# Mixer: the norms' sums of squares of two projection pieces taken by four TensorE column groups at once, from a square tile of twice the size

## The chip, the cores and the metric

The kernel runs on one core of a Trainium2 chip. The core has TensorE (matmuls, from SBUF into PSUM), VectorE, ScalarE, GpSimd and SyncE, which here only starts DMAs. Each engine works through its own list of instructions in order, and the engines meet at semaphores. The metric is the device time of one execution in microseconds, the median of the runs shown. Everything is 32-bit float; in the trace each matmul of this type leaves two weight loads and two MATMUL records.

## The reference, cut to what matters

A decoder layer: x + mixer(norm(x)), then cross attention, then a mixture-of-experts feed-forward. Only the mixer is touched. It is a state recurrence over time, of 4 batches of 1024 tokens:

```python
bc = jnp.einsum('bti,oi->bto', value, W_bc).reshape(Bsz, Tlen, H, 4, N)
bc = bc / (jnp.sqrt(jnp.sum(bc * bc, axis=-1, keepdims=True)) + EPS)
Bz, Bx, Cz, Cx = (bc[..., 0, :], bc[..., 1, :], bc[..., 2, :], bc[..., 3, :])
...
z = S[..., None] * (z - dtE * A[None, :, :, None] * s + dtE * (Bz_t[..., None] * u_t[:, :, None, :]))
s = s + dtE * z + dtE * (Bx_t[..., None] * u_t[:, :, None, :])
y = jnp.einsum('bhn,bhnd->bhd', Cz_t, z) + jnp.einsum('bhn,bhnd->bhd', Cx_t, s)
```

H = 32 heads, N = 32 states, 16 value elements a head. The second line is what the change is about: for every token and head the four vectors Bz, Bx, Cz, Cx are divided by their lengths, for which the sum of squares over the 32 states is needed.

## The kernel before, in words

`attention` first projects the inputs (to about 290 us), then runs `mixer` (to about 2090 us); cross attention and the feed-forward follow. The mixer cuts the 1024 tokens of each batch into 16 time chunks of 64 (u = 0 to 15; 4 batches x 64 tokens = 256 columns, UT) and the heads into 4 groups (gp = 0 to 3). A group of a chunk has the running number n = 4u + gp, 0 to 63.

**Projection in pieces.** The vectors of a group come from `value` in four pieces (i = 0 to 3), running number p = 4n + i. Pieces 0 and 1 are the one half of the group's heads (Bz with Bx, then Cz with Cx), pieces 2 and 3 the other half. `projected` on TensorE writes a piece, 2 x 256 columns, into one of two PSUM slots of `ring` (L603, 8 matmuls). `projected` on ScalarE copies the slot into `bc` (L756) and squares it into `sq` (L759), one tile for all pieces. `summed` on TensorE (L617) multiplies the squares with a selection matrix `sel` that adds up 32 states per head: two matmuls of 256 columns, one for each of the piece's two vectors. Each writes a strip of 32 rows of `ssp`, c = 2(i % 2) + v, so pieces 0 and 2 go to strips 0 and 1, pieces 1 and 3 to strips 2 and 3; the first half of the heads starts the accumulation, the second ends it. A strip of 32 rows is a column group of the array: 128 rows by 32 columns of weights. After piece 3 ScalarE takes root, logarithm and exponential (`norms`, L766 to L770), VectorE multiplies (`factors`, L942), and SyncE sends the factors to DRAM and, spread over the partitions, back into `fb` and `fc`.

**Semaphores of this part.** `ring_full` (a piece is in PSUM), `sq_ready` (it is squared, and the slot is free for piece p + 2), `sums_done` (`sq` may be written again, and the norms may be taken), `nr_root` (the root has read `ssp`, so the next group may start its sums).

**The order of the work.** Each engine's order is written out by hand. On TensorE a group of the loop does: `inputs_turned` (L628, transposes, waits for `in_ready` of VectorE's L969), pieces 0 and 1 of the group three further on, the sum of piece 0, at a chunk's start `outputs` of the chunk before (L690), `causal_products` (L641), piece 2, sum 1, piece 3, sum 2, the first quarter of `mixed_states` (L661), sum 3, the rest of `mixed_states` (L661, L671), `mixed_values` (L681). The sums thus trail the pieces by one, with other work between a projection and its sum. Before the loop the pieces of groups 0 to 2 are projected alone. VectorE works through `evolve` (L916, L922: 64 dependent steps a chunk for the next chunk), `inputs` (L955 to L969), `read_out` (L977 to L994), `mask` (L1002, waits for `causal_products`), `post` (L1014 to L1024, waits for `mixed_values`), in an order of its own, up to two groups ahead of TensorE. SyncE's list of loads follows VectorE's and TensorE's signals (L462 to L507).

Of the kernel before, what the change touches and what calls it, by code (L numbers as in the profile page):

```python
# [10 lines left out]
ACT = mybir.ActivationFunctionType  # L11
AX = mybir.AxisListType

P = 128
B, T, DM = 4, 1024, 256
NTOK = B * T
DI, H, N, DH = 512, 32, 32, 16
# [3 lines left out]
UT = CH * L  # L21
# [310 lines left out]
GP = G // 2  # L332
# [3 lines left out]
def mixer(nc, d, st, wbc, x, x1):  # L336

    with ExitStack() as ctx:
        def sb(name, shape, dt=F32):
            return ctx.enter_context(nc.sbuf_tensor(name, shape, dt))  # L340

        def ps(name, shape):
            return ctx.enter_context(nc.psum_tensor(name, shape, F32))

        def sem(name):
            return ctx.enter_context(nc.semaphore(name))

        ident = sb("ident", [P, P])
        sel = sb("sel", [P, G, H])
# [19 lines left out]
        sg = sb("sg", [P, 4, UT])  # L369
        xs = sb("xs", [P, 2, DM])  # L370
        bc = sb("bc", [P, GP, 4, 2, UT])
        sq = sb("sq", [P, 2, UT])
        nr = sb("nr", [P, UT])
        pq = sb("pq", [P, 2, UT])
        fb = sb("fb", [P, 2, 2, UT])
# [9 lines left out]
        ssp = ps("ssp", [P, 512])  # L385
# [26 lines left out]
        sq_ready = sem("sq_ready")  # L412
        sums_done = sem("sums_done")
# [22 lines left out]
        def turns(v):  # L436

            return v.rearrange("p (t b) -> p t b", b=B)
# [149 lines left out]
        def _(pe):  # L588
# [15 lines left out]
                                       start=(k == 0), stop=(k == 3))  # L604
                mm.then_inc(ring_full, 1)

            def summed(u, gp, i):

                n = GP * u + gp
                p = 4 * n + i  # L610
                g, first = 2 * gp + i // 2, 2 * (i % 2)
                pe.wait_ge(sq_ready, p + 1)
                if i == 0 and n > 0:
                    pe.wait_ge(nr_root, n)
                for v in range(2):
                    c = first + v
                    mm = pe.matmul(ssp[H * c:H * c + H, 0:UT], sel[:, g, :], sq[:, v, :],  # L617
                                   start=(i < 2), stop=(i >= 2))
                mm.then_inc(sums_done, 1)

            def inputs_turned(u, gp):
                n = GP * u + gp
                pe.wait_ge(in_ready, n + 1)
                if n > 0:
                    pe.wait_ge(km_ready, n)
                for v in range(2):
                    for b in range(B):
                        mm = pe.transpose(kp[:, v, b * P:(b + 1) * P],  # L628
                                          turns(bc[:, gp, v].rearrange("p i t -> p (i t)"))[:, :, b], ident[:])
                    mm.then_inc(bt_full, 1)  # L630
# [16 lines left out]
            def mixed_states(u, gp, more, un, gn):  # L647
                n = GP * u + gp
                pe.wait_ge(hpad_ready, 2 * n + 2)
                if gp == 0:  # L650
                    pe.wait_ge(dub_in, 16 * (u + 1))
                    if u > 0:
                        pe.wait_ge(x1_ready, u)
                else:
                    pe.wait_ge(post_ready, n)
                for b in range(B):
                    for i in range(2):
                        for v in range(2):
                            for j in range(J):
                                r = slice(N * j, N * j + N)  # L660
                                pe.matmul(yp[r, b * L:(b + 1) * L], hpad[r, v, i, b, :],  # L661
                                          turns(bc[r, gp, 2 + v, i, :])[:, :, b],
                                          start=(b == 0 and i == 0 and v == 0), stop=False, skip_group_check=True)
                    if b == 0 and more:
                        summed(un, gn, 3)
                for v in range(2):
                    for b in range(B):
                        for j in range(J):
                            q0 = (gp * J + j) * 2 * DH
                            o = yp[N * j:N * j + N, UT + v * P:UT + (v + 1) * P]  # L670
                            pe.matmul(o.rearrange("p (i b e) -> p b i e", i=2, b=B)[:, b],  # L671
                                      btt[:, v, b, N * j:N * j + N], dub[:, b, q0:q0 + 2 * DH],
                                      start=False, stop=True, skip_group_check=True)
# [21 lines left out]
            for gp in range(GP - 1):  # L695
                for i in range(4):
                    projected(0, gp, i)
                    if gp > 0 or i > 0:
                        summed(0, gp - (i == 0), (i - 1) % 4)
            summed(0, GP - 2, 3)  # L700
            for u in range(NU):
                for gp in range(GP):
                    un, gn = (u, GP - 1) if gp == 0 else (u + 1, gp - 1)
                    more = un < NU
                    inputs_turned(u, gp)
                    if more:
                        projected(un, gn, 0)
                        projected(un, gn, 1)
                        summed(un, gn, 0)
                    if gp == 0 and u > 0:  # L710
                        outputs(u - 1)
                    causal_products(u, gp)
                    if more:
                        projected(un, gn, 2)
                        summed(un, gn, 1)
                        projected(un, gn, 3)
                        summed(un, gn, 2)
                    mixed_states(u, gp, more, un, gn)
                    mixed_values(u, gp)
            outputs(NU - 1)  # L720
# [2 lines left out]
        def _(act):  # L723
# [26 lines left out]
            def projected(u, gp, i):  # L750
                n = GP * u + gp
                p = 4 * n + i
                g, first = 2 * gp + i // 2, 2 * (i % 2)
                act.wait_ge(ring_full, p + 1)
                o = ring[:, p % 2, :].rearrange("p (v t) -> p v t", v=2)
                nc.scalar.copy(bc[:, gp, first:first + 2, i // 2, :], o).then_inc(bc_ready, 1)  # L756
                if p > 0:
                    act.wait_ge(sums_done, p)
                nc.scalar.activation(sq[:], o, ACT.Square).then_inc(sq_ready, 1)  # L759

            def norms(u, gp):
                n = GP * u + gp
                act.wait_ge(sums_done, 4 * n + 4)
                if n > 0:
                    act.wait_ge(fac_out, 16 * n)
                nc.scalar.activation(nr[:], ssp[:, 0:UT], ACT.Sqrt).then_inc(nr_root, 1)  # L766
                act.wait_ge(nr_root, n + 1)
                nc.scalar.activation(nr[:], nr[:], ACT.Ln, bias=epsb[:, 0:1]).then_inc(nr_log, 1)
                act.wait_ge(nr_log, n + 1)
                nc.scalar.activation(nr[:], nr[:], ACT.Exp, scale=-1.0).then_inc(nr_ready, 1)  # L770
# [28 lines left out]
            for u in range(NU):  # L799
                for gp in range(GP):  # L800
                    un, gn = (u, GP - 1) if gp == 0 else (u + 1, gp - 1)
# [1310 lines left out]
```

## Time and profile before

| | us |
|---|---|
| median of 3 runs | 3287.18 |
| the runs | 3287.13, 3287.18, 3292.7 |
| the profiled execution | 3292.7 |
| its span, first to last instruction | 3290.8 |
| TensorE busy in the span | 2934.3 (89%) |
| VectorE busy | 2066.6 (63%) |
| ScalarE busy | 1308.5 (40%) |
| mean granted TensorE clock | 0.936 |

The profile is of one execution, and it is the longest of the three shown. Busy times are averages over stages with different limits: the mixer is some 1800 us of the span. TensorE's records overlap, so the time of a block of matmuls is read from its first weight load to the next line's first weight load, not from the durations. Rows that begin with PEld are weight loads, PE the matmuls themselves.

### The profile page before, as it was taken

The numbers are of one execution on the slowest core, as the hardware profiler recorded it, in microseconds if no ns is written. First come the engines' busy times: TensorE is split into PE (matmuls) and PEld (weight loads), VectorE is DVE, ScalarE is ACT, GpSimd is POOL, SyncE is SP. The second block draws the span as 40 slices with busy tenths as digits, with TensorE's granted clock in tenths as the row PEclk, the third lists the DMA queues.
The fourth block names the chain that finished last, engine by engine and source line by source line (L and its number), as shares of the span: only waits on it lengthen the run. The fifth ranks groups of instructions, "written<-read, shape, count | busy, mean of one in ns | idle before, by whom it ended". The sixth has DMA issues, their size and how long they took to land. (4 is left out here: it accounts for less than half of the span.)

```text
span 3290.8 us, 83432 instructions
## 1 busy us (share of the span) xinstructions
PE 2934.3 (89%) x34208; PEld 2179.2 (66%) x34208; DVE 2066.6 (63%) x7109; ACT 1308.5 (40%) x2250; POOL 286.9 (9%) x227
## 2 busy tenths in 40 slices
PE   5885799999999999999999999699888399999997
PEld 2444577777777877787778777433345156888885
DVE  5444998989989988999899889455553000111110
ACT  3443445444545454555444544133331021333332
POOL 0000000000000000000000000000003700433433
PEclk9887899999999999999999999789989599999998
DMA  6556333443353335433543352200052201878777
GB/s 223 157 158 175 92 84 78 129 104 84 78 129 104 82 80 121 113 79 84 129 105 90 73 130 71 74 1 1 1 214 99 99 30 36 207 200 206 205 200 218
DMA packets 249371, 373.92 MB, mean 114 GB/s; under 512 B 54203, under 2 KB 172108, under 8 KB 238156
## 3 DMA queue, kind: packets, MB, share of 16 engines
q1 hardware_dynamic: 226572, 340.18, 37.6%
q0 software_dynamic: 22464, 28.95, 4.3%
q8 instruction: 249, 4.08, 0.5%
q14 instruction: 86, 0.70, 0.1%
HBM read 269.18 MB, written 104.04 MB: 113 GB/s over the span
## 5 line engine op out<-in xcount | busy, mean ns | idle before, releaser
L603 PE MATMUL ring<-valt,wbc 128*128 128x256 f32 x4096 | 945.5, 387 | 29.6 <-DMA valt<-valt_scratch 28.2
L603 PEld LDWEIGHTS ring<-valt,wbc 128*128 128x128 f32 x4096 | 774.5, 193 | 169.3 <-issue 62.9
L756 ACT COPY bc<-ring 128x512 f32<-128x512 f32 x256 | 149.7, 585 | 789.7 <-PE ring L603 789.7
L916 DVE TENSOR_TENSOR uu<-phi,coef 128x64 f32<-128x64 f32 x2048 | 359.4, 215 | 2.1
L922 DVE TENSOR_TENSOR phi<-phi,uu 128x64 f32<-128x64 f32 x2048 | 359.0, 215 | 0.0
L2039 DVE TENSOR_SCALAR f_yr<-fp_y,f_meta 128x256 f32<-128x256 f32 x124 | 54.3, 479 | 414.9 <-PE fp_y L1856 414.9
L661 PE MATMUL yp<-bc,hpad 32*32 32x64 f32 x8192 | 260.4, 289 | 3.9 <-DVE hc L1024 3.9
L661 PEld LDWEIGHTS yp<-bc,hpad 32*32 32x32 f32 x8192 | 225.4, 121 | 54.9 <-issue 54.7
L1923 ACT ACTIVATE f_hT<-fp_h,f_b 128x256 f32<-128x256 f32 x248 | 117.6, 474 | 328.2 <-PE fp_h L1847 328.2
L1856 PE MATMUL fp_y<-f_w,f_hT 128*128 128x256 f32 x992 | 230.7, 386 | 7.9
L1723 POOL DMA_INDIRECT acc_scratch<-f_yr,f_meta x124 | 192.6, 1553 | 445.1 <-DVE f_yr L2039 301.1
L1847 PE MATMUL fp_h<-f_xrt,f_w 128*128 128x256 f32 x992 | 227.0, 382 | 0.8 <-ACT f_xrt L1912 0.8
L1710 POOL COPY f_xn<-f_gk 128x32 f32<-128x32 f32 x3 | 0.7, 244 | 2508.1 <-DVE f_rowid L2020 2504.9
L1856 PEld LDWEIGHTS fp_y<-f_w,f_hT 128*128 128x128 f32 x992 | 183.4, 190 | 45.0 <-ACT f_hT L1923 22.6
L1847 PEld LDWEIGHTS fp_h<-f_xrt,f_w 128*128 128x128 f32 x992 | 190.2, 192 | 27.6 <-issue 1.2
L1972 DVE TENSOR_TENSOR xres<-fp_y,xres 128x1024 f32<-128x1024 f32 x10 | 12.2, 1224 | 266.7 <-remote 131.9
L617 PE MATMUL ssp<-sq,sel 128*32 128x256 f32 x1024 | 160.6, 392 | 8.9 <-ACT sq L759 8.9
L641 PEld LDWEIGHTS kp<-bc 32*64 32x64 f32 x8192 | 140.9, 203 | 32.1 <-issue 32.1
L1764 PE MATMUL fp_y<-f_ws,f_hT 128*128 128x256 f32 x512 | 123.8, 393 | 40.2 <-issue 39.8
L641 PE MATMUL kp<-bc 32*64 32x64 f32 x8192 | 152.7, 305 | 6.8 <-issue 4.4
L759 ACT ACTIVATE sq<-ring 128x512 f32<-128x512 f32 x256 | 153.2, 598 | 0.7 <-PE ssp L617 0.7
L1764 PEld LDWEIGHTS fp_y<-f_ws,f_hT 128*128 128x128 f32 x512 | 100.9, 198 | 67.5 <-issue 55.1
(227 smaller groups left out, 4081.2 us busy)
## 6 DMA issues: line engine op xcount, KB each, us to landing
f_w<-in_W_dram SPq DMA_DIRECT2D x128, 512.0 KB
coef<-par_scratch SPq DMA_DIRECT2D x128, 256.0 KB, 5.9
fb<-fac_scratch SPq DMA_DIRECT2D x256, 128.0 KB, 3.3
fc<-fac_scratch SPq DMA_DIRECT2D x256, 128.0 KB, 4.3
xg_scratch<-f_fill SPq DMA_DIRECT2D x16, 1032.0 KB, 17.4
f_xr<-xg_scratch SPq DMA_DIRECT2D x64, 258.0 KB
vtok_scratch<-p_vtok SPq DMA_DIRECT2D x32, 512.0 KB, 7.0
dub<-vtok_scratch SPq DMA_DIRECT2D x16, 1024.0 KB, 5.6
```

The lines of the kernel that those rows point to most:

```text
L603: mm = pe.matmul(ring[:, p % 2, v * UT:(v + 1) * UT], wbc[:, k, g, first + v, :], valt[:, u % 2, k, :], start=(k == 0), stop=(k == 3))
L617: mm = pe.matmul(ssp[H * c:H * c + H, 0:UT], sel[:, g, :], sq[:, v, :], start=(i < 2), stop=(i >= 2))
L641: mm = pe.matmul(kp[L * i:L * i + L, j, b * L:(b + 1) * L], turns(bc[r, gp, v, i, :])[:, :, b], turns(bc[r, gp, 2 + v, i, :])[:, :, b], st ...
L661: pe.matmul(yp[r, b * L:(b + 1) * L], hpad[r, v, i, b, :], turns(bc[r, gp, 2 + v, i, :])[:, :, b], start=(b == 0 and i == 0 and v == 0), s ...
L756: nc.scalar.copy(bc[:, gp, first:first + 2, i // 2, :], o).then_inc(bc_ready, 1)
L759: nc.scalar.activation(sq[:], o, ACT.Square).then_inc(sq_ready, 1)
L916: made[k] = mark(V.tensor_tensor(uu[:, k].rearrange("p i (g b) -> p i g b", b=B), phi[:, t, ::-1, k, :].rearrange("p i (g b) -> p i g b", ...
L922: ins = V.tensor_tensor(phi[:, t + 1, :, k, :], phi[:, t, :, k, :], uu[:, k], ALU.add)
L1723: pool.indirect_dma_start(acc, bass.IndirectOffsetOnAxis(ap=meta[:, par, a, 0:1].bitcast(I32), axis=0), yr[:, par, a, :], None, compute_op ...
L1764: mm = pe.matmul(yp[:, 2 * (nb % 2) + a // 2, (a % 2) * DM:(a % 2 + 1) * DM], hT[:, e, f, a * P:(a + 1) * P], ws2[:, e, f, :], start=(e == ...
L1847: mm = pe.matmul(hp[:, f, 0:RT], w1[:, par, k, f * P:(f + 1) * P], xrt[:, par, k, :], start=(k == 0), stop=(k == 1))
L1856: mm = pe.matmul(yp[:, par, a * DM:(a + 1) * DM], hT[:, par, f, a * P:(a + 1) * P], w2[:, par, f, :], start=(f == 0), stop=(f == 3))
```

## The change

The tile `sq` gets two slots, and ScalarE squares piece p into slot p % 2. `summed` is called for half a group instead of for a piece: it waits until both pieces of the half are squared and issues four matmuls, strips 0 to 3, from both slots; `sums_done` counts halves. The number of matmuls stays: 256 calls of two become 128 calls of four. In TensorE's list the sum of the first half stands behind piece 2, where sum 1 stood, and the sum of the second half in the first quarter of `mixed_states`, where sum 3 stood; nothing stands behind piece 1 and piece 3.

```diff
-        sq = sb("sq", [P, 2, UT])
+        sq = sb("sq", [P, 2, 2, UT])
...
-            def summed(u, gp, i):
+            def summed(u, gp, half):
 
                 n = GP * u + gp
-                p = 4 * n + i
-                g, first = 2 * gp + i // 2, 2 * (i % 2)
-                pe.wait_ge(sq_ready, p + 1)
-                if i == 0 and n > 0:
+                g = 2 * gp + half
+                pe.wait_ge(sq_ready, 4 * n + 2 * half + 2)
+                if half == 0 and n > 0:
                     pe.wait_ge(nr_root, n)
-                for v in range(2):
-                    c = first + v
-                    mm = pe.matmul(ssp[H * c:H * c + H, 0:UT], sel[:, g, :], sq[:, v, :],
-                                   start=(i < 2), stop=(i >= 2))
+                for i in range(2):
+                    for v in range(2):
+                        c = 2 * i + v
+                        mm = pe.matmul(ssp[H * c:H * c + H, 0:UT], sel[:, g, :], sq[:, i, v, :],
+                                       start=(half == 0), stop=(half == 1))
                 mm.then_inc(sums_done, 1)
...
                     if b == 0 and more:
-                        summed(un, gn, 3)
+                        summed(un, gn, 1)
...
             for gp in range(GP - 1):
                 for i in range(4):
                     projected(0, gp, i)
-                    if gp > 0 or i > 0:
-                        summed(0, gp - (i == 0), (i - 1) % 4)
-            summed(0, GP - 2, 3)
+                    if i == 2:
+                        summed(0, gp, 0)
+                    elif i == 0 and gp > 0:
+                        summed(0, gp - 1, 1)
+            summed(0, GP - 2, 1)
...
                         projected(un, gn, 1)
-                        summed(un, gn, 0)
...
                         projected(un, gn, 2)
-                        summed(un, gn, 1)
+                        summed(un, gn, 0)
                         projected(un, gn, 3)
-                        summed(un, gn, 2)
...
-                if p > 0:
-                    act.wait_ge(sums_done, p)
-                nc.scalar.activation(sq[:], o, ACT.Square).then_inc(sq_ready, 1)
+                if p >= 2:
+                    act.wait_ge(sums_done, p // 2)
+                nc.scalar.activation(sq[:, p % 2], o, ACT.Square).then_inc(sq_ready, 1)
...
-                act.wait_ge(sums_done, 4 * n + 4)
+                act.wait_ge(sums_done, 2 * n + 2)
```

The list of TensorE for one group of the loop (gp other than 0) before the change, from its transposes to the last three quarters of `mixed_states`; "32x256 x2" are two matmuls that write 32 rows by 256 columns:

```order
L628 MATMUL kp<-ident,bc 128x128 x8
L603 MATMUL ring<-valt,wbc 128x256 x16
L617 MATMUL ssp<-sq,sel 32x256 x2
L641 MATMUL kp<-bc 64x64 x64
L603 MATMUL ring<-valt,wbc 128x256 x8
L617 MATMUL ssp<-sq,sel 32x256 x2
L603 MATMUL ring<-valt,wbc 128x256 x8
L617 MATMUL ssp<-sq,sel 32x256 x2
L661 MATMUL yp<-bc,hpad 32x64 x16
L617 MATMUL ssp<-sq,sel 32x256 x2
L661 MATMUL yp<-bc,hpad 32x64 x48
```

There are four blocks of sums, each between lines of another shape. The same place in the changed kernel:

```order
L628 MATMUL kp<-ident,bc 128x128 x8
L603 MATMUL ring<-valt,wbc 128x256 x16
L641 MATMUL kp<-bc 64x64 x64
L603 MATMUL ring<-valt,wbc 128x256 x8
L617 MATMUL ssp<-sq,sel 32x256 x4
L603 MATMUL ring<-valt,wbc 128x256 x8
L661 MATMUL yp<-bc,hpad 32x64 x16
L617 MATMUL ssp<-sq,sel 32x256 x4
L661 MATMUL yp<-bc,hpad 32x64 x48
```

The blocks behind pieces 1 and 3 are gone, L603 now meets L641 and L661 directly, and the two blocks that stay have four matmuls. The lists of ScalarE, VectorE and SyncE keep all their instructions in their order.

## Rows read from the trace of the kernel before

**Rows 1.** The page: the span, and busy tenths in 40 slices of TensorE and VectorE.
```profile
span 3290.8 us, 83432 instructions
...
PE   5885799999999999999999999699888399999997
...
DVE  5444998989989988999899889455553000111110
```
**Rows 2.** Windows: us, busy us (records) of PE, PEld, DVE, ACT, POOL; clock, DMA, GB/s.
```profile
367.00:476.70 109.70, 104.59 (x1760) 84.48 (x1760) 101.81 (x382) 54.61 (x90) 0.00 (x0) 0.95 0.35 84
...
367.00:2012.70 1645.70, 1596.92 (x26849) 1293.91 (x26849) 1509.30 (x5702) 823.36 (x1350) 0.00 (x0) 0.98 0.40 98
```
**Rows 3.** Waits of PE, 290 to 2045 us: total us, times, longest.
```profile
PE kp L628 <- DVE bc L969: 19.4, 1, 19.4
PE yp L671 <- issue: 18.3, 11, 2.7
PE yp L681 <- issue: 18.1, 12, 3.3
```
**Rows 4.** Waits of VectorE in the same stretch.
```profile
DVE bc L955 <- DMA fb<-fac_scratch: 65.1, 27, 4.3
DVE nr L942 <- ACT nr L770: 28.4, 14, 5.4
DVE km L1002 <- issue: 20.1, 7, 3.8
DVE km L1002 <- PE kp L641: 8.3, 6, 2.6
```
**Rows 5.** Timeline around piece 3: start, us, engine, line, count [idle before <- releaser].
```profile
1213.09 3.72 PE L603 MATMUL ring<-valt,wbc 128*128 128x256 f32 x16
...
1216.74 0.63 PE L617 MATMUL ssp<-sq,sel 128*32 128x256 f32 x4
...
1216.85 0.59 ACT L756 COPY bc<-ring 128x512 f32<-128x512 f32 x1 [2.85 <-PE ring L603]
...
1217.30 1.11 PE L661 MATMUL yp<-bc,hpad 32*32 32x64 f32 x32
...
1217.41 0.60 ACT L759 ACTIVATE sq<-ring 128x512 f32<-128x512 f32 x1
...
1218.34 0.14 PEld L617 LDWEIGHTS ssp<-sq,sel 128*32 128x32 f32 x4 [0.21 <-issue]
...
1218.89 2.68 PEld L661 LDWEIGHTS yp<-bc,hpad 32*32 32x32 f32 x96 [0.41 <-issue]
```
**Rows 6.** Waits, whole span: the weight loads of the sums.
```profile
PEld ssp L617 <- issue: 76.7, 254, 0.3
```
**Rows 7.** Timeline: the same group's other matmuls into four strips.
```profile
1221.79 0.73 PE L671 MATMUL yp<-dub,btt 128*32 128x32 f32 x62
...
1222.37 0.63 PE L681 MATMUL yp<-km,dub 128*32 128x64 f32 x30
```
**Rows 8.** Timeline in the start-up: a sum that waits for its square.
```profile
346.42 0.60 ACT L759 ACTIVATE sq<-ring 128x512 f32<-128x512 f32 x1
347.07 0.14 PEld L617 LDWEIGHTS ssp<-sq,sel 128*32 128x32 f32 x4 [1.18 <-ACT sq L759]
```
**Rows 9.** Timeline at two chunks' starts: VectorE's last input, TensorE's first transpose.
```profile
1130.94 0.41 DVE L969 TENSOR_TENSOR bc<-m,fb 128x256 f32<-128x256 f32 x1
...
1135.72 1.11 PE L628 MATMUL kp<-ident,bc 128*128 128x128 f32 x7
...
1353.51 0.41 DVE L969 TENSOR_TENSOR bc<-m,fb 128x256 f32<-128x256 f32 x1
...
1355.96 0.75 PE L628 MATMUL kp<-ident,bc 128*128 128x128 f32 x4
```
**Rows 10.** Timeline: VectorE's waits on the norms and on the causal products.
```profile
1166.36 0.43 DVE L942 TENSOR_TENSOR nr<-nr,pq 128x256 f32<-128x256 f32 x1 [2.12 <-ACT nr L770]
...
1209.05 1.23 DVE L1002 TENSOR_TENSOR km<-kp,causal 128x1024 f32<-128x1024 f32 x1 [2.75 <-issue]
```
**Rows 11.** Windows, columns as in rows 2: around the pause at 425 us.
```profile
422.00:434.00 12.00, 9.22 (x70) 8.02 (x59) 11.87 (x76) 2.96 (x6) 0.00 (x0) 0.86 0.25 76
```

## The prediction, made before the changed kernel ran

> **What bounds the kernel now.** I first looked for the stretch in which the changed lines run. The page's slices [rows 1] show TensorE at 9 tenths in every slice from the sixth to the twenty-fifth, the mixer, and VectorE at 8 or 9 tenths in the same slices. So two engines are nearly full, and the busy shares alone don't say which sets the pace. The table of windows [rows 2] gives the size: from the first `inputs_turned` at 367 us to that of the last time chunk at 2012.7 us are 1645.7 us for 15 chunks of four groups each, 109.7 us a chunk. In that time VectorE is busy 1509.3 us (100.6 a chunk) and stands idle for 136 us, 9.1 a chunk.
>
> Then the waits. TensorE, from 290 to 2045 us, waits for another engine almost only once, 19.4 us for VectorE before the very first group [rows 3]; what is left are pauses of up to about 3 us with no releaser ("issue", 18.3 us before L671, 18.1 us before L681, the largest of them), 2.5 us or so a chunk in all. VectorE does wait [rows 4]: 65.1 us for its factors to come back by DMA, 28.4 us for the norms of ScalarE, which stand behind TensorE's sums, and 20.1 + 8.3 us for the causal products before `mask`. The last three, 56.8 us or 3.8 a chunk, are waits on TensorE's progress. So TensorE's own program is the path from 367 us to the mixer's end, and VectorE follows it with 3.8 us a chunk in hand. Before 367 us it is the reverse: TensorE sat 19.4 us waiting, and nothing that it saves there counts.
>
> **What a block of sums costs.** A group has four blocks, each of two matmuls (four records). One in its surroundings [rows 5]: L617 starts at 1216.74, and the next line, L661, at 1217.30: 0.56 us. The records of the 256 blocks are alike, 254 of them with the same idle of at most 0.3 us before their first weights [rows 6]. Within the 0.56 us there are two passes and the changeover to the next shape.
>
> **How long a block of four takes.** No block with four column groups of 256 columns is in the trace, so I bound it by the rows on either side. One after the other, records of 256 columns follow each other in (3.72 - 0.38) / 15 = 0.223 us [rows 5]; four of them would need 0.223 x 3 + 0.40 = 1.07 us, and L617 shows 0.63, so the two groups already run side by side. For four groups there are L671 and L681, whose results also go to four 32-row strips [rows 7]. L671's 62 records of 32 columns start within 0.73 - 0.20 = 0.53 us, 8.7 ns apart where one at a time would need 0.223 x 32 / 256 = 28 ns: 3.2 at once. L681's 30 records of 64 columns start within 0.41 us, 14 ns apart instead of 56: 3.9 at once. The loss is a fixed few ns a record, so 256 columns are nearer to L681. I take the block of before with two further records in each pass, the whole pass 2 x 8.7 = 17 ns longer by L671's spacing, and since the second pass follows the first on each strip this comes once: 0.57 us for the new block. Ends: 0.57, and, with L671's 3.2 of 4, 0.56 + 0.44 x (4/3.2 - 1) = 0.67; if the two pairs went one after the other, 0.56 + 2 x 0.223 = 1.0.
>
> **Part one: the block behind piece 1 goes.** The first half is now summed behind piece 2, where a block stood already. Between L603 and L641 (or L690 at a chunk's start) 0.56 us vanish. The direct changeover from L603's shape to L641's was never seen; into L617 it costs the same as out of it (the 0.56 us go up to the next weights in any surroundings), so I take one changeover as removed with the block. Saved: 0.56 us a group. The wait on `sq_ready` is now for piece 1 behind piece 2's projection of 3.7 us, and copy and square take 0.57 + 0.60 us: covered.
>
> **Part two: the block behind piece 3 goes, but it was cover.** The second half is summed behind the first quarter of `mixed_states`, in the place of the old fourth block, and that one needs the square of piece 3, which was projected just before. Today [rows 5]: ScalarE copies the piece from 1216.85, squares it from 1217.41 for 0.60 us, done at 1218.01; the sum's weights load at 1218.34. Slack 0.33 us. Without the third block TensorE would be there 0.56 us earlier, 0.23 before the square is done. In the start-up, where TensorE does wait for a square, its weights start 0.05 us after the square's end (346.42 + 0.60, then 347.07) [rows 8]. So the new wait is 0.23 + 0.05 = 0.28 us, and this edit saves 0.56 - 0.28 = 0.28 us. Behind the waiting sums on TensorE stand the other three quarters of `mixed_states`, `mixed_values` and the next group; VectorE waits for `y_full` at their end, a little earlier than before all the same. Bounds: 0.28, and 0.56 if ScalarE somehow were early; nothing makes it so, its copy starts when the ring is full.
>
> **Part three: the larger tile and the fewer signals.** ScalarE's squares now go to two slots, and piece p waits for `sums_done` of the pair before. Its instructions stay as many (256 squares of 0.60 us). Piece 1's square no longer waits for a sum; it had not been held up by one (piece 3, which waits in the same way, shows its square behind its copy without a pause [rows 5]). Piece 2's square waits, as before, for the block behind its own projection, now 0.017 us longer, with no one waiting for that square before the next group. Nothing either way. SyncE and VectorE have the same instructions.
>
> **The sum.** Per group 0.56 + 0.28 - 2 x 0.017 = 0.81 us. Groups whose sums run inside the loop are 61 (64 less the 3 of the start-up, whose gain lies before the 19.4 us wait and is worth nothing). 61 x 0.81 = 49.4 us.
>
> **Does VectorE let it through?** A chunk would take 109.7 - 3.2 = 106.5 us on TensorE. VectorE needs 109.7 - 3.8 = 105.9 us a chunk without its waits on TensorE, DMA waits kept. That holds by 0.6 us. The place where TensorE could wait is the first group of each chunk, `inputs_turned` on L969 [rows 9]: VectorE is done at 1131.35, TensorE gets there at 1135.72, 4.4 us of slack; the least of the chunks after the first is 1353.92 to 1355.96, 2.0 us. VectorE's way to that point is set anew in every chunk by the wait for the norms (2.12 us at 1166.36) and for the causal products (2.75 us at 1209.05) [rows 10]. Upstream of these TensorE gains 0.8 and 2.2 us of its 3.2, so the slack shrinks by 1.0 us (products waited for) to 2.4 us (norms alone), and only one or two chunks go below zero, by under half a us. I take 1 us off: 48 us. The profiled execution took 3292.7 us (span 3290.8), so it would take 3244.7 and the median of 3287.2 would be 3239. The runs shown go from 3287.1 to 3292.7; this width I keep in the range.
>
> **Rivals.**
> (a) Forecast: 48 us, 3239 (spread with the block's price and pauses: 42 to 54 us).
> (b) VectorE becomes the bound. If about half of its 3.8 us a chunk of waits on TensorE turn into DMA waits (dub, factors and coefficients are loaded at moments that move, and the factors' 65 us are DMA latency that a faster TensorE doesn't shorten), a chunk takes 107.8 us: gain 15 x 1.9 = 28 us, 3259. For it: only 0.6 us between the engines. Against: the slack of 2 to 4 us in every chunk.
> (c) Four groups at once pay as L671 does: 0.67 us a block, 61 x 2 x 0.10 = 12 us less, gain 36, 3251.
> (d) Four groups don't run side by side, two pairs follow each other: each block +0.43, a group saves 0.84 - 0.87, nothing: 3289.
> (e) No wait at the second half: 61 x 1.08 = 66 us, at most what VectorE admits (57 us): 3230.
> (f) Slower: the 0.28 us wait in each group, on top of a changeover, is taken as a pause and the granted clock falls each time. A fall's price: the 12 us around the pause at 425 us ran at 0.86 [rows 11], 12 x 0.14 = 1.7 us of work lost. 61 times is 104 us, less 48: slower by 56, 3343. It decides from the length of pause that draws a fall: that one followed one of the "issue" pauses of up to 3.3 us [rows 3], while the hundreds of changeovers with 0.3 us before L617's weights [rows 6] stand in a stretch granted 0.98 of the clock [rows 2]. A wait of 0.28 us on top of one is nearer to these.
>
> On (c) the Trainium skill has a figure of its own. Its page "TensorE: Matmul & The Clock Gate", in the section "Part 3: Packing small matmuls — row/col tiling", puts three column tiles at 2.38 times one tile's throughput and not at three, and four row tiles at 3.07. Taken for four column groups this would put the block at 4/3.07 = 1.3 times the 0.44 us of its two passes, 0.69 us in all, an estimate from that page, and the gain near 34 us, 3253. L681's 3.9 of 4 speaks against it at this case's own rates.
>
> **Chances.** (a) 0.68, (b) 0.10, (c) 0.08, (d) 0.05, (e) 0.05, (f) 0.02, other 0.02. The range must leave at most 0.2 out: 3228 to 3257 holds (a), (c), (e) and part of (b). This kernel's measurement can tell about 0.2%, 6.6 us, from no change. Faster by more than that: (a), (b), (c), (e), 0.92; within: (d), 0.05; slower: 0.03.
>
> **What the profile after would show.** L617 with 1024 records in 128 blocks of eight, 0.57 us from its first weights to the next line's; (c) and (d) show there first, as 0.67 or 1.0. Before the second half's block a new TensorE wait, L617 on ScalarE's `sq` (L759), 61 times about 0.07 to 0.3 us beyond the changeover. The chunk at 106.5 us. VectorE's waits for the norms and causal products down from 3.8 us a chunk to about 1 and TensorE's for L969 at a chunk's start still near nothing; if the latter comes to 1 us or more a chunk, (b) holds. Everything behind the mixer shifted and unchanged. I am wrong on the step of part two if that wait is missing, and on part one if the direct changeover L603 to L641 takes longer than the 0.3 us between last matmul and next weights.

## The result, and the profile after

The changed kernel took 3250.6 us, median of 4 runs (3238.6, 3250.2, 3251.0, 3251.7), against 3287.5 of the kernel before (3287.1 to 3292.7, 4 runs): ratio 0.9883, interval 0.9855 to 0.9911, a gain of 37 us. Two more comparisons, each within one chip, gave 0.9886 (0.9849 to 0.9922) and 0.9884 (0.9855 to 0.9912). One run of the kernel before, on the chip of the experiments with less on VectorE, took 8392 us at a granted clock of 0.339 and is left out. The forecast was 3239 us in a range of 3228 to 3257.

The page after, span and the slices that answer to [rows 1]:

```profile
span 3249.9 us, 83432 instructions
...
PE   5885699999999999999999998698887399999996
...
DVE  5444999999999998899999998455452000111110
```

The mixer is shorter by half a slice; both engines are as full as they were. The window from the first group to the first of the last chunk, answering to [rows 2]:

```profile
365.20:1968.20 1603.00, 1538.11 (x26849) 1279.59 (x26849) 1504.56 (x5694) 814.66 (x1350) 0.00 (x0) 0.98 0.40 100
```

1603.0 us for 15 chunks instead of 1645.7: 42.7 us less, 106.9 us a chunk. This stretch, from the first chunk's start to the last one's, is called the loop below. The span is 40.9 us shorter: 42.7 in the loop, some 2 us by an earlier start, and a last chunk and feed-forward some 3.5 us longer (1281.8 us from the loop's end to the span's, against 1278.2; a second trace has 1274.6). VectorE's busy time is the same to 5 us.

The place of [rows 5] in the changed kernel, from the timeline of TensorE and of ScalarE (start, us, engine, line, count):

```profile
1138.89 1.11 PE L661 MATMUL yp<-bc,hpad 32*32 32x64 f32 x32
1140.14 0.64 PE L617 MATMUL ssp<-sq,sel 128*32 128x256 f32 x8
1140.71 2.96 PE L661 MATMUL yp<-bc,hpad 32*32 32x64 f32 x96
...
1139.00 0.59 ACT L756 COPY bc<-ring 128x512 f32<-128x512 f32 x1 [3.02 <-PE ring L603]
1139.48 0.60 ACT L759 ACTIVATE sq<-ring 128x512 f32<-128x512 f32 x1
```

The block has eight records and runs from 1140.14 to 1140.71: 0.57 us, against 0.56 with four [rows 5]; to three digits it is 0.569 against 0.556 in the groups of the loop, so two more groups of 256 columns cost 0.013 us. The square is done at 1140.08 (1139.48 + 0.60), the sum's weights follow 0.05 us later. The waits of TensorE's weight loads on the sums, 290 to 2000 us, show the new wait in every group:

```profile
PEld ssp L617 <- ACT sq L759: 37.8, 64, 10.7
PEld ssp L617 <- issue: 21.2, 64, 0.3
```

64 blocks wait for a square, 64 don't; before, 254 of 256 didn't [rows 6]. From the start of L661's last matmul record to L617's weights it is now 0.42 us where it was 0.22 (read record by record, alike in all 61 groups): a wait of 0.20 us.

TensorE's waits between the two ends of the loop, answering to [rows 3] (total us, times, longest). A row "issue" has no releaser in the profile and is called a pause; the others are waits for another engine:

```profile
PE yp L681 <- issue: 16.5, 10, 3.5
PE yp L671 <- issue: 15.4, 10, 4.8
PE kp L641 <- issue: 10.3, 6, 4.7
PE kp L628 <- DVE bc L969: 5.0, 4, 2.7
PE kp L628 <- issue: 4.4, 3, 1.9
PE yp L681 <- DVE km L1002: 2.1, 1, 2.1
PE kp L641 <- ACT btt L778: 1.4, 1, 1.4
PE yp L690 <- DVE hc L1024: 0.8, 2, 0.4
PE ring L603 <- issue: 0.7, 1, 0.7
```

The pauses come to 47.3 us, as before (47.0). The waits for the other engines come to 9.3 us, where they were 1.5; 5.0 of them are at the chunk starts. VectorE's waits, answering to [rows 4]:

```profile
DVE bc L955 <- DMA fb<-fac_scratch: 53.7, 25, 3.5
DVE nr L942 <- ACT nr L770: 12.4, 9, 3.1
DVE km L1002 <- PE kp L641: 9.4, 8, 2.5
DVE km L1002 <- issue: 4.1, 2, 2.4
```

Its waits on TensorE's progress fell from 56.8 us (53.2 of them in the loop) to 25.9 us, 1.7 a chunk, where about 1 was forecast.

So TensorE's list should have shortened by 4 x 0.556 - 2 x 0.569 - 0.20 = 0.89 us a group, 53 us in the loop's 60 groups, and 42.7 came through. Where the other 10 stayed is the question of the experiments.

### The profile page after: what moved, and what is told of

Read it like the earlier page. It is cut to its first block and busy times, and to the rows that moved or that the text cites. A ratio compares the mean times of both kernels' runs of the same rounds, so it can differ in the third digit from the quotient of the medians.

```text
span 3249.9 us, 83432 instructions
## 1 busy us (share of the span) xinstructions
PE 2870.0 (88%) x34208; PEld 2165.1 (67%) x34208; DVE 2067.0 (64%) x7109; ACT 1299.5 (40%) x2250; POOL 287.0 (9%) x227
## 5 line engine op out<-in xcount | busy, mean ns | idle before, releaser
L603 PE MATMUL ring<-valt,wbc 128*128 128x256 f32 x4096 | 947.1, 388 | 28.8 <-DMA valt<-valt_scratch 28.1
L603 PEld LDWEIGHTS ring<-valt,wbc 128*128 128x128 f32 x4096 | 777.7, 194 | 166.7 <-issue 58.9
L916 DVE TENSOR_TENSOR uu<-phi,coef 128x64 f32<-128x64 f32 x2048 | 367.1, 223 | 2.1
L922 DVE TENSOR_TENSOR phi<-phi,uu 128x64 f32<-128x64 f32 x2048 | 367.3, 223 | 0.0
L661 PE MATMUL yp<-bc,hpad 32*32 32x64 f32 x8192 | 260.4, 289 | 5.2 <-DVE hc L1024 5.0
L661 PEld LDWEIGHTS yp<-bc,hpad 32*32 32x32 f32 x8192 | 225.5, 122 | 51.3 <-issue 51.2
L1847 PEld LDWEIGHTS fp_h<-f_xrt,f_w 128*128 128x128 f32 x992 | 190.0, 192 | 27.5 <-issue 1.2
L641 PE MATMUL kp<-bc 32*64 32x64 f32 x8192 | 154.3, 306 | 15.7 <-issue 11.9
L641 PEld LDWEIGHTS kp<-bc 32*64 32x64 f32 x8192 | 142.0, 203 | 37.8 <-issue 37.8
L1879 ACT ACTIVATE f_hT<-fp_h,f_bs 128x512 f32<-128x512 f32 x64 | 43.4, 687 | 204.3 <-remote 106.2
```

The costliest lines, as they stand in the source:

```text
L603: mm = pe.matmul(ring[:, p % 2, v * UT:(v + 1) * UT], wbc[:, k, g, first + v, :], valt[:, u % 2, k, :], start=(k == 0), stop=(k == 3))
L641: mm = pe.matmul(kp[L * i:L * i + L, j, b * L:(b + 1) * L], turns(bc[r, gp, v, i, :])[:, :, b], turns(bc[r, gp, 2 + v, i, :])[:, :, b], st ...
L661: pe.matmul(yp[r, b * L:(b + 1) * L], hpad[r, v, i, b, :], turns(bc[r, gp, 2 + v, i, :])[:, :, b], start=(b == 0 and i == 0 and v == 0), s ...
L916: made[k] = mark(V.tensor_tensor(uu[:, k].rearrange("p i (g b) -> p i g b", b=B), phi[:, t, ::-1, k, :].rearrange("p i (g b) -> p i g b", ...
L922: ins = V.tensor_tensor(phi[:, t + 1, :, k, :], phi[:, t, :, k, :], uu[:, k], ALU.add)
L1847: mm = pe.matmul(hp[:, f, 0:RT], w1[:, par, k, f * P:(f + 1) * P], xrt[:, par, k, :], start=(k == 0), stop=(k == 1))
```

## The experiments

### The change once more

> The changed kernel once more, for its spread (3238.6 to 3251.7 us so far) and a second trace. Theory A (TensorE's own list is the path, the missing 11 us of the loop are pauses and waits that differ from run to run): the block of four is again 0.57 us, the loop's sum of TensorE pauses and waits goes with the time, so a run that is 10 us shorter shows 10 us less of them. Theory B (VectorE sets the pace now): TensorE waits for VectorE at the chunk starts by about 0.8 us a chunk or more, and the time repeats within 2 us. A: somewhere from 3236 to 3252. B: 3250.

Measured 3244.0 us (3238.9 to 3260.1), before on the same chip 3284.1. The spread of single runs is 20 us, also for the kernel before (3272 to 3291): theory B's 2 us is wrong as far as the whole time goes. In these four runs most of the spread goes with the granted clock: their spans lie 21 us apart, and multiplied by their mean clock (0.930 to 0.936) they are 3028.8 to 3033.9 us. And the loop repeats: 1603.8 us here, 1603.0 above. TensorE's waits in it:

```profile
PE kp L628 <- DVE bc L969: 13.9, 8, 2.8
PE yp L681 <- issue: 11.6, 14, 3.5
PE kp L641 <- issue: 10.7, 4, 4.6
PE yp L671 <- issue: 8.5, 7, 3.3
PE kp L641 <- ACT btt L778: 6.8, 5, 1.7
```

With the smaller rows the pauses are 34.3 us, 13 less than in the first trace, and the waits for VectorE and ScalarE 24.7 us, 15 more. TensorE had fewer pauses and stood waiting for the other engines instead. Theory A, by which 13 us fewer pauses make the loop 13 us shorter, is wrong; B's 0.8 us a chunk at the starts is met here (13.9 / 15 = 0.9), though not in the first trace (5.0 / 15 = 0.3).

### Each half alone

> Part one alone: the first half of a group is summed by one block of four, the second half by two blocks of two as before. By the rows of both kernels a group saves 2 x 0.556 - 0.569 = 0.54 us, 61 groups 33 us. A: 3254 us, and this part and the other one alone add up to about 54 us. B (VectorE lets through only some 37 us in all): each part alone still gives nearly all of its share, so that their sum is well above the 37 us of both together; a split of 37 us in proportion (23 us, 3264) would speak against both and for blocks that are worth less than they look.

```diff
                         projected(un, gn, 3)
+                        summed_piece(un, gn, 2)
                     mixed_states(u, gp, more, un, gn)
...
-                        summed(un, gn, 1)
+                        summed_piece(un, gn, 3)
```

`summed_piece` is the old block of two, and the signals are counted anew. Measured 3250.4 us (3240.5 to 3263.1), ratio 0.9895 (0.9858 to 0.9932); loop 1613.2 us, 32.5 less than before, by 33 expected. This half comes through whole, in part by chance: the trace has 6.7 us fewer pauses than the one of before, and 4.9 us more waits for other engines.

> Part two alone: the second half by one block of four behind the first quarter of L661, the first half by two blocks as before. A group saves 0.54 us less the wait for piece 3's square, which the changed kernel's trace shows as 0.42 - 0.22 = 0.20 us: 0.34 us, 61 groups 21 us. A and B: 3267 us. If the wait weren't there: 33 us, 3254. The prediction's size, 0.28 a group: 17 us, 3270.

```diff
                         projected(un, gn, 1)
+                        summed_piece(un, gn, 0)
...
                         projected(un, gn, 2)
-                        summed(un, gn, 0)
+                        summed_piece(un, gn, 1)
```

Measured 3279.4 us (10 runs, 3266.3 to 3291.6), ratio 0.9977 (0.9959 to 0.9995): 5 to 8 us where 21 were expected. The loop took 1638.9 us, 6.8 less than before. Record by record its blocks are as forecast: the sums (L631 in this kernel) at 0.42 us behind the first quarter of `mixed_states`, 0.57 us long. Its waits are

```profile
PE yp L695 <- issue: 23.6, 12, 3.4
PE yp L685 <- issue: 15.3, 10, 3.0
```

(L695 and L685 are L681 and L671 in this kernel), 50.9 us of pauses with the smaller rows instead of 47.0. That explains 4 of the missing 14 us, and waits of 3.0 us instead of 1.5 another 1.5. By the clock records of the traces TensorE was granted 1.2 GHz for 70 us of this loop and for 51 us of the one before, 65 and 49 of them while it worked; 16 us at half the rate are another 8. With these the 14 us are found, in this trace. They are what the traces show beside the change, not something that the edit is known to cause, and with medians so far from 21 us in 10 runs I can't call it chance either. The sum of the two parts alone, 33.7 + 4.7 = 38 us by medians, is that of both together (40 us), not 54: not what either theory said. In TensorE's own list the two do add up, as the table in the next section shows.

### The wait taken away

> The changed kernel with ScalarE's copy and square of a piece exchanged (the ring slot is then given free by the copy). Piece 3's square is done some 0.5 us earlier, so the 0.20 us wait before the second block goes. A: 61 x 0.20 = 12.5 us less than the changed kernel, 3238 us, and 0.22 us between L661 and L617. B: the wait goes too, but VectorE doesn't follow: 3250 us, and TensorE waits longer at the chunk starts, by some 0.8 us a chunk more.

```diff
-                nc.scalar.copy(bc[:, gp, first:first + 2, i // 2, :], o).then_inc(bc_ready, 1)
                 if p >= 2:
                     act.wait_ge(sums_done, p // 2)
                 nc.scalar.activation(sq[:, p % 2], o, ACT.Square).then_inc(sq_ready, 1)
+                nc.scalar.copy(bc[:, gp, first:first + 2, i // 2, :], o).then_inc(bc_ready, 1)
```

and `projected` on TensorE waits for `bc_ready`. Measured 3242.4 us (3228.0 to 3248.3), the changed kernel beside it 3244.0: no difference that can be told, and with four runs each, spread over 20 us, 12.5 us can't be excluded either. The 0.20 us wait is gone from all groups (0.22 us between L661 and L617 again), and the loop is 1601.0 us, 2.8 shorter instead of 12.5. It went into these:

```profile
PE kp L628 <- DVE bc L969: 23.4, 8, 4.9
PE kp L641 <- issue: 13.0, 4, 4.8
PE yp L681 <- issue: 10.9, 13, 3.0
```

With the smaller rows 31.9 us of waits for other engines beside 31.5 us of pauses. TensorE was given 12 us and waits 7 us longer for the other engines than in the second trace (9.5 us longer for L969), which is theory B. Another 5.5 us went to the clock, which neither theory had: TensorE worked at a granted 1.2 GHz for 57 us of this loop, for 46 us in the second trace. Span times mean clock is 3016 to 3024 us in the four runs here, against 3029 to 3034 in those of the changed kernel, so the 12 us are gone from the work in every run.

### Less on VectorE

> The kernel before with less on VectorE: of the 8 running sums over time that accumulate (L934) takes per chunk, 6 are left out, some 3.6 us of VectorE a chunk by the 4.79 us that the eight take; this leaves part of the computation out, the decays come out as they are before the sum. Theory A (before the change TensorE's list is the path): same time as before, about 3284 us, from the first to the last chunk's start still some 1645 us. Theory B (VectorE already shares the path): shorter by up to 54 us.

```diff
-                    for b in range(B):
+                    for b in range(1):
                         ins = V.tensor_tensor_scan(v[:, :, b], resetm[:], v[:, :, b], 0.0, ALU.mult, ALU.add)
```

> The changed kernel with the same 6 of 8 running sums left out of each chunk on VectorE. TensorE's own work from chunk start to chunk start fell by about 60 us less the 0.2 us waits, 53 us, of which 42 came through. A (the rest is fetch-like pauses and the slower clock on TensorE itself, random in place): no gain over the changed kernel, 3244 to 3250. B (the rest went into waits of TensorE on VectorE at the chunk starts, L628 on L969): these waits go to nothing and the time falls by some 10 us, to about 3235, so that before and after with a light VectorE differ by about 50 us.

Measured 3272.3 us (10 runs, ratio to before 0.9965, 0.9945 to 0.9986) and 3216.9 us (3208.7 to 3218.5, ratio 0.9794, 0.9752 to 0.9837). Both versions leave part of the computation out, as their expectations say. By medians the change is worth 55 us when VectorE is light and 37 to 40 us when it isn't. In the light version of the changed kernel TensorE no longer waits at the chunk starts:

```profile
PE yp L671 <- issue: 17.3, 12, 2.7
PE yp L681 <- issue: 15.5, 12, 2.8
PE kp L628 <- issue: 4.3, 3, 2.4
PE kp L641 <- issue: 4.2, 4, 2.1
PE yp L681 <- DVE km L1002: 1.4, 1, 1.4
```

L969 is gone from the list, as B said; VectorE's last input is ready 2.2 to 5.7 us ahead of TensorE at each of the 15 later chunk starts. But the loop is 19.6 us shorter than in the changed kernel, not 10: only 7.9 us of that are waits, 5.3 are pauses and 6.6 the clock. The loops of these two traces are less clear than the medians, too:

```profile
363.50:1990.40 1626.90, 1589.93 (x26849) 1288.09 (x26849) 1458.61 (x5612) 822.00 (x1350) 0.00 (x0) 0.99 0.40 99
```
```profile
360.90:1944.30 1583.40, 1531.68 (x26849) 1274.98 (x26849) 1457.40 (x5610) 814.42 (x1349) 0.00 (x0) 0.99 0.41 102
```

The first row is before, the second after, both light: 43.5 us apart, not 53. And the kernel before became some 13 us shorter by a lighter VectorE (19 us in the loop) although TensorE waited for VectorE only 1.5 us in its loop. In the trace that gain is 11 us less of pauses (35.6 against 47.0) and 33 us granted at 1.2 GHz against 51, which is 8 us (the windows say 0.99 against 0.98 [rows 2]). Why a lighter VectorE should bring fewer pauses I don't know; one trace of each can't tell it from chance.

> Square ahead of copy, and 6 of the 8 running sums a chunk left out on VectorE. With the copy first, taking the 0.2 us wait away gave 12.5 us of TensorE's time back and only some 2 us of it came through, with 31.8 us of TensorE waits, most of them for VectorE's L969. B: with a light VectorE those 12 us come through, about 3223 us, loop some 1580 us. A: 3240.

Measured 3213.7 us (3211.1 to 3215.7) against 3216.9 of the copy first: 3 us, not 12. Loop 1576.6 us against 1583.4: 6.8 of the 12.5 us, where the heavy VectorE let 2.8 through. TensorE waits for other engines by only 1.9 us in this loop, so what is missing here isn't VectorE's: it worked at 1.2 GHz for 48 us instead of 39, which is 4.6 us, and paused for 42.7 us instead of 42.0. By the whole time B isn't confirmed; by the loop it is in part.

### VectorE's own pace

> The changed kernel with a quarter of the projection left out (three of four row blocks are summed): 4 x 2 matmuls fewer a group, 16 records of 0.22 us, 3.5 us a group and 14 us a chunk less on TensorE. So VectorE with its own waits for DMA sets the pace, and the loop shows its floor. The prediction had 105.9 us a chunk, 1588 us for 15. If B holds already in the changed kernel, the floor is near what the changed kernel takes, 1600 us; if VectorE had room, 1560 to 1590.

```diff
-                    for k in range(4):
+                    for k in range(3):
                         mm = pe.matmul(ring[:, p % 2, v * UT:(v + 1) * UT], wbc[:, k, g, first + v, :], valt[:, u % 2, k, :],
-                                       start=(k == 0), stop=(k == 3))
+                                       start=(k == 0), stop=(k == 2))
```

Measured 3226.0 us (3220.3 to 3227.3), with a quarter of the projection left out. The loop:

```profile
363.20:1951.40 1588.20, 1378.93 (x25889) 1130.52 (x25890) 1503.22 (x5694) 813.32 (x1350) 0.00 (x0) 0.92 0.41 101
```

Some 210 us of TensorE's work are gone, and the loop is only 15 us shorter than in the changed kernel. TensorE waits for L969 in each of the 15 chunk starts:

```profile
PE kp L628 <- DVE bc L969: 77.2, 15, 6.5
```

VectorE waits for TensorE's progress by only 5.6 us here. So 1588 us, 105.9 a chunk, is VectorE's pace with its waits for DMA (60.7 us in this trace; they range from 53.7 to 65.3 in the changed kernel's). It is the figure that the prediction worked out.

### The multiplication of the norms moved off VectorE

Since VectorE has no room, I moved its smallest separable piece to the idle GpSimd, in both kernels and with the square first.

> The kernel before with the 64 multiplications of the norms by the row factors (L942) moved from VectorE to GpSimd, which has nothing to do in the mixer. VectorE loses 64 x 0.43 us and its waits for the norms (28.4 us) and part of its waits for the factors' DMA (65 us), since the factors start as soon as ScalarE has them. Theory B (both engines share the path once TensorE is shortened, before it TensorE's list alone): near the kernel with the lighter VectorE, which gained 14 us: 3270 us. Theory A (VectorE is never the path): no change.

> The changed kernel with the same move to GpSimd. Nothing is left out. B: the 53 us that TensorE's list gave up come through whole, as with the light VectorE: near 3217 to 3225 us, TensorE's waits at the chunk starts (L628 on L969) gone. A: as the changed kernel, 3244 us. Slower than that if GpSimd's work on SBUF holds VectorE up.

> The same with the square ahead of the copy, which takes the 0.20 us wait of the second block away. B: up to 12.5 us less than with the copy first, if VectorE has the room now: 3205 to 3220 us. A: 3238.

> The changed kernel beside the three others, for comparison on one chip: 3240 to 3250 us.

```diff
+        @block.gpsimd
+        def _(pool):
+            for n in range(GP * NU):
+                if n % GP == 0:
+                    pool.wait_ge(pq_in, 48 * (n // GP + 1))
+                pool.wait_ge(nr_ready, n + 1)
+                nc.gpsimd.tensor_tensor(nr[:], nr[:], pq[:, n // GP % 2, :], ALU.mult).then_inc(fac_ready, 1)
```

All on one chip, whose feed-forward is some 90 us faster than the others' (778.6 us from its first transpose to the end in the changed kernel, 870.3 in the second trace): before 3187.5; before with the move 3192.7, ratio 1.0017 (0.9998 to 1.0035); the changed kernel 3148.9; with the move 3167.6, ratio to before 0.9941 (0.9919 to 0.9962); with the square first as well 3164.1. For the kernel before, the "no change" of theory A is met and B's 14 us are not. For the changed kernel neither theory is met: the move costs it 19 us, 12.5 of them in the loop (1616.8 against 1604.3 us). What happened is the last sentence of the expectation, that GpSimd's work holds VectorE up. On GpSimd the multiplication takes 1.98 us in the mean where VectorE took 0.43, but its time isn't fixed (least, median and longest in ns):

```profile
L826 POOL TENSOR_TENSOR nr<-nr,pq x64: 724/998/7613, 323.7 to 2013.9; 128x256 f32<-128x256 f32 x64
```

The eight longest, 4.6 to 7.6 us, all ran beside VectorE's long instructions of `inputs` and `read_out`; the eight shortest, 0.72 to 0.73 us, beside its short steps of `evolve` or beside nothing. And the other way round: 28 instructions of VectorE in this loop took over 0.4 us longer than the median of their line, 15 us in sum, each of them beside a multiplication on GpSimd; the changed kernel has none. The running sums show it, with the move and without:

```profile
L942 DVE TENSOR_TENSOR_SCAN pinv<-resetm,pinv x128: 656/667/1223, 338.0 to 1961.8; 128x256 f32<-128x256 f32 x128
```
```profile
L934 DVE TENSOR_TENSOR_SCAN pinv<-resetm,pinv x128: 655/670/695, 337.3 to 1948.6; 128x256 f32<-128x256 f32 x128
```

So the two engines hold each other up. VectorE's busy time fell by only 5 us of the 26 that the multiplications took, and its waits for the factors, which come later, grew (in the loop 78 + 12 us against 63 + 3 in the changed kernel on the same chip):

```profile
DVE bc L956 <- DMA fb<-fac_scratch: 77.6, 27, 6.2
DVE bc L956 <- ACT bc L756: 11.5, 2, 6.2
```
```profile
DVE bc L955 <- DMA fb<-fac_scratch: 62.8, 26, 4.6
DVE bc L955 <- ACT bc L756: 2.9, 1, 2.9
```

The first of these two is with the move, the second without. The changed kernel's loop was 1604.3 us here, the third time within 1.3 us, with 31.3 us of pauses and 27.5 us of waits for the other engines. None of the versions that compute the whole result beats the changed kernel by more than the measurement can tell.

## Why the prediction was right, and where its size was off

**The direction and most of the size** follow from the block. It was put at 0.57 us by L681's four strips at once, and it takes 0.569. The direct changeovers from L603 to L641, L661 and L690, never seen before, take 0.31 us from the start of the last matmul record to the next weights, like those through L617. (c) and (d) are refuted in the first trace (0.57 us), (f) by the clock of the loop (0.98 as before) and the time, and so is the estimate from the Trainium skill's page "TensorE: Matmul & The Clock Gate", section "Part 3: Packing small matmuls — row/col tiling", by which the block would take 0.69 us. Case (a), which had 0.68 of the chances, has the right mechanism, but the gain of 37 us lies under its own 42 to 54. The time fell on the figure of (c), 3251 us, whose mechanism is refuted: that is luck. The range held the result because it was drawn to take in (c) and part of (b).

**The wait** was put at 0.28 us and is 0.20. The step that failed is the sentence that piece 3's square had never been held up by a sum. [rows 5] show it: copy at 1216.85, square at 1217.41, 0.56 us apart, just when the sum that started at 1216.74 ended its 0.63 us. Now copy and square of that piece start 0.48 us apart in all 61 groups, before they started 0.57 apart in all. The square was waiting for `sq` by 0.08 us in every group, and the second slot gave that back. With it TensorE's list lost 53 us in the loop's 60 groups instead of 49.

**"Does VectorE let it through"** is the term that was mis-sized: I took 1 us off, and in the loop 10 to 12 stayed behind. The floor was right (105.9 us a chunk worked out, 105.9 measured), though the 3.8 us taken off came from a longer stretch than the loop; the loop's own 53.2 us would have given 106.2. The pauses were put at 2.5 us a chunk in all and were 3.1 (47.0 / 15): 2.5 is the two largest rows alone. The error is the step from two averages to a sum: TensorE at 106.5 and VectorE at 105.9 were compared as if each chunk took its mean. TensorE alone (light VectorE) needs 1583 us, VectorE alone 1588, and together they take 1603, in three traces within 1.3 us, while TensorE's pauses went from 31 to 47 us. As I read it, a pause of 3 to 5 us delays VectorE, and where there is none TensorE overtakes and waits: with 47, 34 and 31 us of pauses, VectorE waited 26, 18 and 20 us for TensorE, and TensorE 9, 25 and 28 us for the others. No run sets the pauses by itself. The slack at L969 that I took as 2.0 to 4.4 us less 1.0 to 2.4 became nothing at several chunk starts: TensorE waited there in 4, 8 and 9 of them. This is rival (b) in part, at 10 us instead of its 20. By the prediction's own sign, 1 us a chunk or more at L969, (b) holds in one of the three traces (0.3, 0.9 and 1.3 us a chunk).

**Where the time went, loop by loop.** The traces can be put side by side in us: the pauses and the waits for other engines (idle stretches of over 0.15 us), and the cost of the lower clock, which is half of the time that TensorE worked at a granted 1.2 GHz (there an L603 record takes up to 0.80 us, else 0.38). What is left of the loop is TensorE's own list at the full clock.

| kernel | loop | pauses | waits | low clock | left |
|---|---|---|---|---|---|
| before | 1645.7 | 47.0 | 1.5 | 24.4 | 1572.8 |
| before, light VectorE | 1626.9 | 35.6 | 1.2 | 16.3 | 1573.8 |
| first half only | 1613.2 | 40.3 | 6.4 | 25.5 | 1541.0 |
| second half only | 1638.9 | 50.9 | 3.0 | 32.2 | 1552.8 |
| changed | 1603.0 | 47.3 | 9.3 | 25.9 | 1520.5 |
| changed, second trace | 1603.8 | 34.3 | 24.7 | 23.1 | 1521.7 |
| changed, third trace | 1604.3 | 31.3 | 27.5 | 24.4 | 1521.1 |
| changed, light VectorE | 1583.4 | 42.0 | 1.4 | 19.3 | 1520.7 |
| square first | 1601.0 | 31.5 | 31.9 | 28.6 | 1509.0 |
| square first, light VectorE | 1576.6 | 42.7 | 1.9 | 23.9 | 1508.1 |

The last column repeats within 1.5 us for a kernel, whatever the rest does, and each edit shows in it whole: 52 us for the change (53 worked out), 32 and 20 for its halves (32.6 and 20.6 for 60 groups), 12 to 13 for the square first (12.0). The halves do add up. What doesn't come through of the change's 52 us in the first trace is 7.8 us of waits and 1.5 of clock; in the other two 23 and 26 us of waits, less 13 and 16 us of pauses.

What stays open: why the sum of pauses, waits and clock comes out as it does. Nobody set the pauses or the clock by an edit, and a lighter VectorE changed both (the gain of 55 us by medians is 43.5 in the loops of single traces). The changed kernel's mean clock over a whole run is also lower on the third chip, 0.948 in 6 runs against 0.952 in 24 of the kernel before, some 10 us at most; its loops don't show that (50 to 59 us at 1.2 GHz, before 51), so where it lies isn't known.

**The median** hid more than it showed: the changed kernel's loop repeats within 1.3 us in three traces, single runs spread by 20 us. The two errors also partly cancel: the list lost 4 us more than forecast, and 10 less came through. With medians of four runs the forecast can't be judged to better than some 10 us.

## What to carry to other kernels

Matmuls that use one strip of the array each can be cheap to put together: here a block with four strips took 0.569 us, one with two 0.556. Count blocks and changeovers, not matmuls. Before removing a block, look for what ran under it; here half a microsecond of sums was the cover of the next square. When the bounding engine is shortened to within some per cent of the second one, don't take the larger of two averages: expect to lose something in every chunk where the chunks differ. In the first trace of the changed kernel they took 102.7 to 111.3 us, and 0.7 us a chunk was lost (0.8 in the other two). And split a loop's time into work, pauses, waits and clock before explaining a difference: the work alone repeated to 1.5 us. Before moving work to an idle engine, look whether the two hold each other up; moving 60 multiplications of 0.43 us off VectorE made the loop 12.5 us longer.

## What the runs showed of the hardware

TensorE's pauses without a releaser each end at the same distance from a transfer of the instruction queue. Over the loops of all fourteen traces, 283 pauses of over 0.6 us end 2.2 to 3.7 us after the start of such a packet of 16 KB, all but seven of them no more than 3.0 us after it. There is such a packet every 7.5 to 7.8 us on average, and 2.2 to 3.0 us behind one lies only a tenth of the loop, so this isn't chance. One of the longest of the changed kernel, 4.66 us before L641:

```profile
507.48 2.33 PE L641 MATMUL kp<-bc 32*64 32x64 f32 x127 [1.45 <-ACT btt L778]
514.47 0.38 PE L641 MATMUL kp<-bc 32*64 32x64 f32 x1 [4.66 <-issue]
```

and the DMA queues from 511.9 to 513.4 us; it is the first packet of that queue to start since 498.9:

```profile
q8 instruction: 1, 0.02, 3.7%
```

This reads as TensorE waiting for its own instructions, behind the stretches of short matmuls (L661, L671, L681). It was not tested by an experiment. It is 31 to 51 us of the loops in the table.

The clock falls follow idle time of TensorE. In the loops of four traces (before, changed twice, square first) there are 49 falls to 1.2 GHz, and the last idle stretch before each (of those over 0.15 us) was 1.1 to 4.9 us long, a pause or a wait for another engine. Not every such stretch is followed by a fall: one of 2.3 us in the kernel before isn't. So a wait for VectorE may cost clock as well as its own length.
